# Decoder layer on one core: GpSimd multiplies the second row tile of each softmax group, and the steps stand in a new order

## What is computed

```python
# reference, cut
x = x + attn(layernorm(x))            # 16 heads of 32; softmax(q k^T) v, then Wff, + bff
x = x + xattn(ctx, ctx, layernorm(x)) # one head of 512 over 750 context rows
x = x + ffn(layernorm(x))             # top-8 of 2048 scores, softmax, weighted sum of values, gate

# attn, the part that the change touches
scores = einsum('bqhd,bkhd->bhqk', q, k)
attn = softmax(scores, axis=-1)
out = einsum('bhqk,bkhd->bqhd', attn, v).reshape(B, S, D) @ Wff.T + bff
```

## Time and profile before

| | us |
|---|---|
| median of 3 runs | 3028.26 |
| lowest and highest | 3023.71, 3029.1 |
| the profiled execution's own time | 3032.06 |
| its span, first to last instruction | 3030.2 |
| busy PE, of the span | 92% |
| busy DVE, of the span | 71% |
| busy ACT, of the span | 49% |
| busy POOL, of the span | 24% |

### The profile page before, as it was taken

One profiled execution on the slowest core, in us unless ns is written; L12 is line 12 of the kernel. 1 busy time (PEld: TensorE's weight loads), 2 busy tenths in 40 slices (PEclk: granted clock), 3 DMA queues, 4 the chain that ended last, 5 costly groups with the idle time before them and its releaser, 6 DMA issues.

```text
span 3030.2 us, 56150 instructions
## 1 busy us (share of the span) xinstructions
PE 2773.7 (92%) x18911; PEld 2092.0 (69%) x18911; DVE 2162.0 (71%) x4148; ACT 1498.3 (49%) x4403; POOL 740.0 (24%) x619
## 2 busy tenths in 40 slices
PE   8699999999999999999999999999999999999500
PEld 4567777777777777777777777777777777776300
DVE  3445777877777777887777777777777777786543
ACT  1346555555555555555555555555555555554200
POOL 0001222222222222222222222222222223232310
PEclk8899999999999999999999999999999999999755
DMA  4101222322222222222222222232222222222299
GB/s 151 39 22 42 70 92 81 92 84 84 84 75 88 70 85 87 87 87 83 82 80 85 72 81 87 87 93 78 87 85 77 74 76 88 86 88 82 76 324 312
DMA packets 106523, 280.40 MB, mean 93 GB/s; under 512 B 14401, under 2 KB 14449, under 8 KB 102481
## 3 DMA queue, kind: packets, MB, share of 16 engines
q1 hardware_dynamic: 57842, 147.71, 15.4%
q0 software_dynamic: 40960, 117.47, 13.4%
q10 hardware_dynamic: 7680, 14.68, 1.3%
HBM read 235.77 MB, written 44.04 MB: 92 GB/s over the span
## 4 chain that ended last, share of the span: by engine, by line
PE 73%; DVE 12%; issue 6%; ACT 3%; SPq 3%; DMA 2%; DVEq 1%; POOL 0%; ACTq 0%
PE psX L874 30%; PE psA L874 19%; PE psA L883 6%; PE psF L874 6%; PE psX L883 5%; PE psA L934 4%; ACT pa L487 3%; PE psA L957 2%; DVE top L764 2%; SPq L386 2%; SPq L387 1%; DVE nmax L697 1%; DMA agg_scratch<-agg 1%; DVE idx L767 1%; DVE stats_A L609 1%
## 5 line engine op out<-in xcount | busy, mean ns | idle before, releaser
L427 POOL DMA_INDIRECT vg<-in_L_ffn_aux_values,idx x512 | 494.6, 966 | 1744.3 <-DVE agg L789 972.0
L487 ACT ACTIVATE pa<-psA,nmax 112x224 f32<-112x224 f32 x1024 | 443.7, 448 | 194.5 <-DVE nmax L697 191.0
L789 DVE SCALAR_TENSOR_TENSOR agg<-vg,wt,agg 112x512 f32<-112x512 f32 x448 | 395.7, 883 | 18.0 <-DMA vg<-in_L_ffn_aux_values,idx 8.9
L874 PE MATMUL psX<-big,gT 128*112 128x375 f32 x1024 | 336.2, 480 | 2.3 <-ACT nx L526 1.8
L697 DVE TENSOR_REDUCE nmax<-psA 112x4 f32<-112x896 f32 x256 | 266.8, 1084 | 99.6 <-PE psA L934 99.6
L874 PE MATMUL psX<-pT,cx 125*128 125x224 f32 x1536 | 304.9, 355 | 0.0
L874 PEld LDWEIGHTS psX<-pT,cx 125*128 125x128 f32 x1536 | 286.1, 190 | 3.9
L710 DVE TENSOR_TENSOR pa<-pa,rsum 112x896 f32<-112x896 f32 x256 | 279.5, 1092 | 9.5 <-DVE rsum L708 0.3
L874 PEld LDWEIGHTS psX<-big,gT 128*112 128x112 f32 x1024 | 177.4, 176 | 132.1 <-ACT nx L526 2.4
L451 ACT COPY paT<-psA 112x448 f32<-112x448 f32 x512 | 238.7, 548 | 12.2 <-PE psA L883 7.7
L874 PE MATMUL psX<-wffT,oT 128*112 128x512 f32 x512 | 227.7, 598 | 17.1 <-ACT oT L451 17.1
(11 more groups left out here) (186 smaller groups left out, 5813.8 us busy)
## 6 DMA issues: line engine op xcount, KB each, us to landing
cx<-in_ctx SPq DMA_DIRECT2D x32, 1500.0 KB
xa<-in_x SPq DMA_DIRECT2D x32, 448.0 KB, 5.8
xr<-in_x SPq DMA_DIRECT2D x32, 448.0 KB, 5.0
base_scratch<-x SPq DMA_DIRECT2D x32, 448.0 KB, 3.1
agg_scratch<-agg SPq DMA_DIRECT2D x64, 224.0 KB, 3.3
vg<-in_L_ffn_aux_values,idx POOLq DMA_INDIRECT x512, 3.4
m<-base_scratch SPq DMA_DIRECT2D x8, 448.0 KB, 14.8
m<-agg_scratch SPq DMA_DIRECT2D x8, 448.0 KB, 16.8
```

The source lines that it names most:

```text
L427: pool.indirect_dma_start(vgv[:, c % SLOTS, k, :], None, aux_values, bass.IndirectOffsetOnAxis(ap=idx[:, t, n:n + 1], axis=0))\
L487: last = nc.scalar.activation(pa[:, t, h, :], psA[0:R, h, t * S:(t + 1) * S], ACT.Exp, bias=nmax[:, k % 2, h, t:t + 1], accum_out=rsum[:, ...
L789: last = nc.vector.scalar_tensor_tensor(agg[:, :], vgv[:, c % SLOTS, k, :], w, agg[:, :], ALU.mult, ALU.add)
L874: last = nc.tensor.matmul(dst, stationary, moving, start=n == 0, stop=n == len(pairs) - 1)
```

## The change

In `share` DVE still takes both reciprocals, but multiplies only tile 0. The multiplication of tile 1 is a new function `share_last` on GpSimd, which waits for the reciprocal (the step count of stream A on DVE). The semaphore `a_shared` becomes one for each tile, and PE waits for that of the tile it turns. The table `ORDER` is another.

```diff
-        a_maxed, a_exped, a_shared, x_maxed = sem("a_maxed"), sem("a_exped"), sem("a_shared"), sem("x_maxed")
+        a_maxed, a_exped, x_maxed = sem("a_maxed"), sem("a_exped"), sem("x_maxed")
+        a_shared = [sem(f"a_shared{t}") for t in range(T)]
...
+            def share_last(b, k):
+                pool.wait_ge(steps["A"], A_STEPS * b + A_STEPS - T * (NB - 1 - k))
+                t = T - 1
+                nc.gpsimd.tensor_tensor(pa[:, t, :, :], pa[:, t, :, :],
+                                        rsum[:, k, t, :].unsqueeze(2).to_broadcast([R, HB, S]), ALU.mult)\
+                    .then_inc(a_shared[t], 1)
...
-            pipeline(pool, {("A", "mix"): bias_x, ("X", "norm"): bias_x1, ("F", "norm"): add_base,
+            pipeline(pool, {("A", "share"): share_last, ("A", "mix"): bias_x, ("X", "norm"): bias_x1, ("F", "norm"): add_base,
...
                     mark("A", nc.vector.reciprocal(rsum[:, k, t, :], rsum[:, k, t, :]))
+                    if t == T - 1:
+                        break
                     settle("A", b)
...
-                                            ALU.mult).then_inc(a_shared, 1)
+                                            ALU.mult).then_inc(a_shared[t], 1)
...
-                    pe.wait_ge(a_shared, T * (NB * b + k) + t + 1)
+                    pe.wait_ge(a_shared[t], NB * b + k + 1)
...
-    ("X", "norm", 0), ("G", "sum", 1), ("A", "qk", 0), ("A", "value", 0), ("X", "turn", 0), ("A", "score", 0),
-    ("G", "sum", 2), ("A", "share", 0), ("F", "norm", 0), ("X", "query", 0), ("A", "prob", 0), ("A", "qk", 1),
...
+    ("F", "norm", 0), ("A", "share", 0), ("X", "query", 0), ("A", "qk", 1), ("G", "sum", 2), ("A", "qk", 2),
+    ("X", "ctx", 2), ("A", "prob", 0), ("G", "sum", 3), ("F", "turn", 0), ("X", "ctx", 3), ("A", "score", 1),
```

## The result

The changed kernel takes 3131.62 us (median of 4 runs, 3129.3 to 3132.6), the kernel before beside it 3028.68 (3023.71 to 3033.85): a ratio of 1.034 [1.032, 1.036]. It is 3.4% slower. The forecast was 3108 in a range of 3050 to 3140. One iteration of the loop takes 88.77 us, against 84.93: 3.84 more, where 2.5 were forecast.

A forecast was written before the change was run, and what follows sets the result against it. PE, busy 92% of the span, was taken as the bound. Five stretches summed to 87.45 us, +2.5 an iteration: +75 over 30 iterations, +5 for the first two, giving 3112, less 3.8: 3108 us, range 3050 to 3140.

The forecast's parts named there:

- P to Q: End of A score 0 to end of A score 1: 17.7 us against 16.17, prob 0's fourth fill 1.65 late.
- E to P: X enter's start to end of A score 0: 19.8 us, at most 20.1; qk_lo 0 about 1.0 later, nearly covered.
- The clock: PE's granted clock: 1.00 in all five windows of the iteration, so it has nothing to give.
- Q to U: End of A score 1 to end of A score 2: 21.7 us against 22.85, prob 1's fourth fill 0.9 late.
- U to V: End of A score 2 to end of A score 3: 14.6 us against 12.90, POOL's multiplication hidden.
- V to E: End of A score 3 to X enter's start: 13.65 us against 13.22; PE waits 1.1 for paT before mix 3.
- the wait for oT: At X enter on PE: the 0.55 us wait disappears under X out 1.
- qk_lo is free: DVE's qk_lo beside a POOL operation: not held; if held, it adds 0.6 us an iteration.
- rival 4: Worse: qk_lo held, POOL at 2.37, or further places (bias_x before G sum 6): +3.4 and more, 3140 to 3160; chance 0.08.
- Rivals 1 to 3: Turns better at one place: 3060 to 3085, 0.14; no exclusion: 3030 to 3045, 0.06; faster: 2990 to 3000, 0.10.
- The sum: The five stretches of one iteration together: 87.45 us, +2.5 an iteration.
- 5 added for the first iterations: Iterations 0 and 1: no cover for four multiplications that are 1.0 us longer, +5 us.

The follow-up runs named there:

- experiments 3 and 4: Changed kernel with G sum 0 back ahead of X enter: 3093.69 us, 1.021; changed kernel with POOL's bias_x1 addition one head group later: 3074.83 us, 1.015.
- experiment 1: Kernel before with the new order table alone, all multiplications still on VectorE: 3125.73 us, ratio 1.032.
- experiment 2: Changed kernel with the old order table, so only the multiplications moved to GpSimd: median 3132.06 us of three of four runs, ratio 1.035.

## Why the prediction was right, and where not

- **P to Q, 17.7 forecast, 17.71 measured, for another reason.** The mechanism (POOL's multiplication holds G sum 2, qk_lo 2 comes late, the last four turns of prob 0 wait) was sound: experiments 3 and 4 show it with 1.26 us, where I had 1.65. The difference is POOL's 1.68 us against my 2.07, by 0.4. In the changed kernel it shows in only one of 28 iterations; in the others PE comes 1.68 late by the clock. What I hadn't seen is that the new order makes DVE as late without POOL (experiment 1): the hold takes the place of the multiplication that it moved away. The agreement to 0.01 is chance; a table of stretches alone would have passed it as proof.
- **E to P, the step that failed.** "DVE reaches qk_lo 0 about 1.0 later, which the distance ... nearly covers": it was 2.2. I had seen that L413 and a G sum exclude each other, but priced it for the large multiply-adds, and forgot the 112x8 scaling ahead of them, which is held for the whole 2.40 us. That 0.23 us of work can cost 2.40 was legible in the earlier trace rows, where the copy of 112x2 took 0.64 beside L418. I had even named the small operations, and then counted only those with two tensors.
- **The clock** wasn't in the sum at all. I had written that it has nothing to give; that was true, but it had 1.68 us to take. Of these only 0.46 are net here, since without them prob 0 waits. A new wait of PE can cost more than its length when the clock falls behind it.
- **Q to U**: prob 1's fourth fill waits 0.44, not 0.9, since POOL is faster by 0.4; the length fits within 0.16. **U to V** 14.58 against 14.6. **V to E** 13.66 against 13.65, with 1.07 for paT against 1.1, and the wait for oT gone as forecast.
- **qk_lo is free** beside POOL, as I took it from L658. The Trainium skill, "SBUF — State Buffer", section "Who interferes with whom", draws the line at two SBUF inputs; qk_lo (0.62 beside L415) agrees. The same section also says that copies and TENSOR_SCALAR operations can enter a two-port mode, when their operands meet its conditions, and then contend, whoever is first blocking the other. The scaling is such an operation, and its 2.40 us agree, though no run shows in which mode it ran. So do L666's copy in the earlier trace rows and, in experiment 2, the TENSOR_SCALAR of 112x2 that took 1.62 beside a multiplication. I had quoted the exception ("outside the two-port modes") and not asked which small instructions it takes in.
- **Of the rivals**, rival 4 ("worse, further places") came nearest in time, and by its last clause: a further place, though at bias_x1 and not at bias_x. Rivals 1 to 3 didn't happen; the relief of DVE brought nothing, since PE waited for it almost nowhere.
- **The sum**: 87.45 forecast, 88.77 measured. The loop's 28 iterations at +3.84 make 107 us; the time ahead of it and behind it is together 8 us shorter than before, which gives the 99 us of the two profiled executions. I had 80, with 5 added for the first iterations, where nothing was to be added.

## What to carry to other kernels

Work moved to an engine whose instructions hold up those of its old one, and are held up by them, must be priced with both queues side by side, down to the smallest instruction: one of 0.23 us that starts 0.02 behind a long one costs the long one's length. Where PE is the bound, reckon with what the clock may take behind each new wait, and look what the wait covers: a removed stall uncovers the next (here 3.43 us went and 1.26 came back). And measure rivals side by side: the changed kernel and the one with the late bias addition differed by 1.8% on the first chip and by nothing on the third.

## What the runs showed of the hardware

- Right after an idle time of 1.64 to 1.71 us in front of the scores TensorE was granted 0.50 of its clock, 1.2 GHz, for about 3.4 us in 27 of 28 iterations of the changed kernel, in 15 of 28 of experiment 1 and in 6 of 28 of the changed kernel on the third chip; after one of 1.05 in prob 0 it stayed at 1.00 in experiments 3 and 4. So the same wait doesn't bring the same clock each time, and which iterations escape stays open. On the third chip the waits of 0.39, 0.87 and 1.27 us, one close behind the other in prob 0, also brought it down, with the late bias addition:

```profile
1528.00:1530.00 2.00, 0.73 (x5) 0.51 (x6) 1.96 (x4) 0.53 (x1) 0.00 (x0) 0.75 0.00 0
1530.00:1532.00 2.00, 2.00 (x12) 2.00 (x12) 1.14 (x2) 0.97 (x2) 1.68 (x2) 0.50 0.14 16
```

- GpSimd multiplies 112x896 by a broadcast column in 1.68 us, VectorE in 1.09; GpSimd's addition of 112x1024 with a row broadcast over the tile takes 2.37. Between these two the cost isn't in proportion to the columns.
- Three chips gave one program 3028, 3062 and 3059 us, and another 3075 on the first and 3209 on the third. Between the first and the third, instructions of VectorE and GpSimd took the same time; on the second and third, a further gap of 1.4 to 2.8 us in VectorE's queue goes with GpSimd's gather issues. Its cause stays open.
